# Binary-activation convolution: thresholds moved from VectorE to GpSimd, eviction order and a PSUM bank changed

## The chip, the cores and the metric

The kernel runs on one core of a Trainium2 chip. The metric is the device time of one execution in microseconds. The kernel before took 206.68 us, the median of 3 runs (206.48 to 207.05). Engines are called PE (TensorE), DVE (VectorE), ACT (ScalarE), POOL (GpSimd) and SP (the DMA issuer).

## The reference

`x` has the shape 32 x 56 x 56 x 32 (images, height, width, channels), fp32. Each channel of each image is normalised over its 56 x 56 positions. The 3x3x32x32 filter is replaced by a sum of five sign filters, whose weights `alpha` solve a 5x5 least-squares system. Three sign activations of the normalised input, with thresholds shifted by `v[n]`, are convolved with it, scaled by `beta[n]`, summed, and added to the input:

```python
mean, std = jnp.mean(W), jnp.sqrt(jnp.var(W))
B = jnp.sign(W[None] - mean + us[:, None, None, None, None] * std)      # 5 sign filters
alpha = jnp.linalg.solve(Bf.T @ Bf, Bf.T @ wf)
W_eff = jnp.einsum('m,mhwio->hwio', alpha, B)
for n in range(3):
    An = jnp.sign(jnp.clip(X + v[n], 0.0, 1.0) - 0.5)                   # X: x normalised per image and channel
    out = out + beta[n] * (conv(An) + sum(alpha) * bias[n])
return x + out
```

The sign of `clip(X + v, 0, 1) - 0.5` is the sign of `x` minus a threshold per image and channel. So the kernel never writes the normalised input; it needs a mean, a deviation and three thresholds for every image and channel.

## The kernel before

The 32 images are 16 pairs. A pair is loaded with its 112 rows (2 images x 56) on the partitions and transposed on PE, so that four columns x 32 channels lie on the partitions. Each pair has two halves of blocks, 8 and 6; a half fills two PSUM banks of `x_ps`, `y_ps` or `conv_ps[f]` with 448 or 336 columns each.

For a pair, in this order:
- PE transposes x (`bring_in`, L685), ACT copies it to `x_ch` (`copy_in`, L343).
- DVE takes statistics per lane (L555, L562) and spreads them (L565). PE gathers them over the four lanes of a channel with one matmul (`gather_lanes`, L693), DVE aggregates the result to moments (L573), ACT takes the root (L353), DVE makes the reciprocal and three thresholds (L577 to L591).
- ACT takes the signs for activations 1, 2, 0 (L348), each in two instructions, one per image.
- DVE weighs the signs of activations 1 and 2 with high parts of the ratios of beta (L599, L601), adds them (L605), and adds the signs of activation 0 (L612). POOL weighs them with low parts (L306, L310), and DVE adds these (L617).
- SP copies the sums by DMA to `s_odd`, shifted over the partitions. PE convolves them (`convolve`, L723, L726, L731).
- ACT evicts with a scale (`scale_out`, L361), PE transposes back (`bring_out`, L743), DVE adds x and a constant (L546), SP stores.

Every engine runs a list written out by hand, `step(p)` for p from -2 to 15; in one step pair p is finished, pair p+1 begins its convolution, pair p+2 is summed, pair p+3 gets its thresholds and first signs, and pair p+4 is brought in. Engines meet by semaphores only. The order on PE is convolve(p, 1), bring_out(p, 0), bring_in(p+4, 0), gather_lanes(p+3), convolve(p+1, 0), bring_out(p, 1), bring_in(p+4, 1). On ACT it is signs 2 of p+2, scale_out(p, 1), signs 0 of p+2, root of p+3, both copies of p+4, signs 1 of p+3, scale_out(p+1, 0).

Ahead of the steps stand the filter's own work (mean, signs, Gram matrix, elimination, `filter_parts` at L501) and the order of the activations by the size of beta on POOL (`order_beta`, L249; `split_ratios`, L277). The parameters beta, v and bias come by three DMAs that broadcast them to 128 partitions. `filter_parts` weighs the five sign filters one after another (L506 to L516).

The gathered statistics `stat_ps` lie in columns 464 to 487 of the first bank of `x_ps`.

Of the kernel before, what the change touches and what calls it, by code (L numbers as in the profile page):

```python
# [36 lines left out]
def preact_conv_kernel(nc, x, w, beta, v, bias, out):  # L37
    ctx = ExitStack()
    with ctx:
# [28 lines left out]
        twice_dev = sb("twice_dev", [128, 2])  # L68
# [8 lines left out]
        eps_col = sb("eps_col", [128, 1])  # L77
        params = sb("params", [128, 3, N_ACT])
# [21 lines left out]
        size = sb("size", [128, 3])  # L100
        w_eff = sb("w_eff", [128, TAPS, 2, C])
# [22 lines left out]
        root_ready = sem("root_ready")  # L124
        thr_ready = sem("thr_ready")
# [19 lines left out]
        bias_loaded = sem("bias_loaded")  # L145
# [86 lines left out]
        def _(pool):  # L232
# [16 lines left out]
            def order_beta():  # L249

                pool.wait_ge(params_loaded, 32)
# [66 lines left out]
            weigh_low(0)  # L318
            pool.wait_ge(lo_weighed, 2)
# [5 lines left out]
            for q in range(1, PAIRS):  # L325
                weigh_low(q)

        @block.scalar
        def _(act):
            load_filter(act, 1)  # L330
            act.dma_start(params[:, 1, :], v.partition_broadcast(128)).then_inc(params_loaded, 16)
            act.dma_start(params[:, 0, :], beta.partition_broadcast(128)).then_inc(params_loaded, 16)
            act.dma_start(params[:, 2, :], bias.partition_broadcast(128)).then_inc(bias_loaded, 16)
# [30 lines left out]
            def begin_signs(q):  # L364
                act.wait_ge(thr_ready, 3 * (q + 1))
# [9 lines left out]
            def step(p):  # L375
# [4 lines left out]
                if real(p + 2):  # L380
                    sign(p + 2, 0)
                if real(p + 3):
                    take_root(p + 3)
                if real(p + LEAD):
                    copy_in(p + LEAD, 0)
                    copy_in(p + LEAD, 1)
                if real(p + 3):
                    begin_signs(p + 3)
                if p == -1:
                    act.wait_ge(y_scale_ready, 1)  # L390
                if real(p + 1):
                    scale_out(p + 1, 0)

# [10 lines left out]
            copy_in(1, 0)  # L404
            copy_in(1, 1)
            begin_signs(0)
# [4 lines left out]
        def _(dve):  # L411
# [89 lines left out]
            def filter_parts():  # L501
                neg_w = w_eff[:].rearrange("p a o c -> p (a o c)")
                fl = [filt[:, :, :, :, m].rearrange("p a o c -> p (a o c)") for m in range(M_FIL)]
# [5 lines left out]
                mark(nc.vector.reciprocal(size[:, 1:2], size[:, 0:1]))  # L509
# [12 lines left out]
                dve.wait_ge(bias_loaded, 16)  # L522
                dve.wait_ge(params_loaded, 32)
# [51 lines left out]
            def invert_root(q):  # L575
                dve.wait_ge(root_ready, q + 1)
                return mark(nc.vector.reciprocal(inv_root[:], root[:]))  # L577

            def divide_variance(q, n):
                dve.wait_ge(moments_ready, 2 * (q + 1))  # L580
                settle(n)
                return mark(stt(twice_dev[:], moments[q % 2][:, :, 1], GN_EPS, inv_root[:], ALU.add, ALU.mult))  # L582

            def add_root(n):
                settle(n)
                return mark(tt(twice_dev[:], twice_dev[:], root[:], ALU.add))

            def make_thresholds(q, n):
                settle(n)
                for m in range(N_ACT):  # L590
                    stt(neg_thr[q % 2][:, m, :], twice_dev[:], order[:, 1, m:m + 1], moments[q % 2][:, :, 0],  # L591
                        ALU.mult, ALU.subtract).then_inc(thr_ready, 1)

            def thresholds(q):
                make_thresholds(q, add_root(divide_variance(q, invert_root(q))))
# [23 lines left out]
            def step(p):  # L619
# [10 lines left out]
                if real(r):  # L630
                    make_thresholds(r, add_root(divide_variance(r, invert_root(r))))
# [14 lines left out]
            filter_bias()  # L646
            lane_moments(0, 0)
# [4 lines left out]
            dve.wait_ge(divisor_ready, 1)  # L652
            nc.vector.reciprocal(tmp[:, 5, 2:3], tmp[:, 5, 1:2]).then_inc(inverse_ready, 1)
            dve.wait_ge(order_ready, 3)
            thresholds(0)
# [158 lines left out]
```

## Time and profile before

| | |
|---|---|
| median of the runs | 206.68 us |
| profiled execution | 206.35 us, span 204.6 us |
| PE busy | 167.0 us, 82% |
| DVE busy | 171.6 us, 84% |
| ACT busy | 139.9 us, 68% |
| POOL busy | 62.7 us, 31% |
| chain that ended last | PE 49%, ACT 19%, DVE 16%, issue 7%, DMA 6% |

The span is the time from the first to the last instruction of the profiled execution; the execution's own time is longer by 1.75 us. Busy shares are averages over a start of some 45 us, a middle in which all engines repeat a period, and a tail of some 40 us. The chain that ended last is followed back from the last instruction, at each step to what released it.

### The profile page before, as it was taken

The page shows a single profiled execution, that of the slowest core. Times are in us where ns is not written, and L with a number is a line of the kernel's source. Part 1 is how long each engine was busy: PE and PEld are TensorE (multiplying, and loading weights), DVE is VectorE, ACT ScalarE, POOL GpSimd, SP SyncE. Part 2 cuts the span into 40 slices and gives each one's busy share as a digit, 9 for nine tenths or more (in the row PEclk, how much of TensorE's full clock was granted, in tenths as well). Part 3 has the DMA queues.
Part 4 walks back from the last instruction along what each step waited for, and adds up shares of the span by engine and source line. Part 5 has one row for each costly group of instructions (what it writes and reads, how often), then busy time and mean ns, then how long its engine had stood idle before and what let it go on. Part 6 is the DMA issues. An engine that isn't in the chain of part 4 may idle for free.

```text
span 204.6 us, 4766 instructions
## 1 busy us (share of the span) xinstructions
PE 167.0 (82%) x1800; PEld 128.9 (63%) x1800; DVE 171.6 (84%) x422; ACT 139.9 (68%) x183; POOL 62.7 (31%) x76
## 2 busy tenths in 40 slices
PE   1596166489898989898989898989899999789871
PEld 0484065266767676767676767777777776658560
DVE  5449999998999999999999999999999999875241
ACT  2626557287888878787878787878787878673110
POOL 6174243543333333232323232414141414240000
PEclk9999999999999999999999999999999999999998
DMA  4799333061688979797889787978797464657625
GB/s 113 228 268 272 94 81 85 0 163 51 193 233 240 265 215 262 212 256 221 239 240 262 216 254 226 255 224 253 227 251 229 131 187 137 181 149 211 194 67 157
DMA packets 21030, 39.61 MB, mean 194 GB/s; under 512 B 9744, under 2 KB 9744, under 8 KB 21008
## 3 DMA queue, kind: packets, MB, share of 16 engines
q1 hardware_dynamic: 20272, 39.27, 67.9%
q8 instruction: 14, 0.23, 0.5%
q10 hardware_dynamic: 736, 0.04, 0.2%
q14 instruction: 8, 0.07, 0.1%
HBM read 13.15 MB, written 12.85 MB: 127 GB/s over the span
## 4 chain that ended last, share of the span: by engine, by line
PE 49%; ACT 19%; DVE 16%; issue 7%; DMA 6%; SPq 2%; ACTq 0%; DVEq 0%
PE conv_ps L723 24%; PE y_ps L743 13%; ACT signs L348 13%; PE x_ps L685 9%; ACT y_ch L361 6%; DMA x_nat<-in_x 4%; DMA s_odd<-s_even 3%; DVE raw_stats L555 2%; DVE y_nat L546 2%; DVE twice_dev L582 1%; DVE s_even L612 1%; DVE s_even L617 1%; PE x_ps L693 1%; DVE neg_thr L591 1%; PE conv_ps L782 1%
## 5 line engine op out<-in xcount | busy, mean ns | idle before, releaser
L723 PE MATMUL conv_ps<-s_even,w_mm 128*64 128x448 f16 (+1 forms) x576 | 102.9, 332 | 3.0 <-DVE w_mm L518 1.6
L726 PE MATMUL conv_ps<-s_odd,w_mm 128*64 128x448 f16 (+2 forms) x576 | 102.9, 320 | 0.0
L348 ACT ACTIVATE signs<-x_ch,neg_thr 128x784 f16<-128x784 f32 x96 | 85.0, 940 | 2.2 <-DVE neg_thr L591 2.2
L723 PEld LDWEIGHTS conv_ps<-s_even,w_mm 128*64 128x64 f16 x576 | 60.5, 110 | 30.4 <-issue 5.0
L726 PEld LDWEIGHTS conv_ps<-s_odd,w_mm 128*64 128x64 f16 x576 | 60.6, 110 | 0.0
L546 DVE SCALAR_TENSOR_TENSOR y_nat<-y_ps,y_const,x_nat 112x1024 f32<-112x1024 f32 (+1 forms) x32 | 36.6, 1145 | 10.2 <-PE y_ps L743 10.2
L306 POOL TENSOR_SCALAR lo_part<-signs,ratio_lo 128x1568 f16<-128x1568 f16 x16 | 25.5, 1595 | 62.3 <-ACT signs L348 62.2
L685 PE MATMUL x_ps<-ident,x_nat 112*128 112x112 f32 x224 | 31.8, 290 | 13.4 <-ACT x_ch L343 10.1
L743 PE MATMUL y_ps<-ident,y_ch 128*112 128x128 f32 x224 | 31.2, 279 | 11.3 <-ACT y_ch L361 9.9
L310 POOL TENSOR_SCALAR lo_part<-signs,ratio_lo 128x1568 f16<-128x1568 f16 x16 | 26.6, 1664 | 44.9 <-DVE half_hi L605 44.9
L343 ACT ACTIVATE x_ch<-x_ps 128x896 f32<-128x896 f32 (+1 forms) x32 | 26.1, 815 | 19.5 <-PE x_ps L685 19.5
L361 ACT ACTIVATE y_ch<-conv_ps,y_scale 128x896 f32<-128x896 f32 (+1 forms) x32 | 28.9, 904 | 11.3 <-PE conv_ps L726 6.2
L685 PEld LDWEIGHTS x_ps<-ident,x_nat 112*128 112x128 f32 x224 | 27.1, 159 | 14.4 <-issue 12.1
L743 PEld LDWEIGHTS y_ps<-ident,y_ch 128*112 128x112 f32 x224 | 23.4, 133 | 20.0 <-ACT y_ch L361 12.6
L555 DVE BATCH_NORM_STATS2 raw_stats<-x_ch 128x6 f32<-128x448 f32 (+1 forms) x64 | 31.6, 553 | 4.0 <-ACT x_ch L343 4.0
L731 PE MATMUL conv_ps<-s_odd,w_edge 128*64 128x112 f16 x144 | 22.5, 214 | 0.0
L612 DVE TENSOR_TENSOR s_even<-half_hi,signs 128x1568 f16<-128x1568 f16 x16 | 19.6, 1226 | 0.0
L353 ACT ACTIVATE root<-moments,eps_col 128x2 f32<-128x2 f32 x16 | 4.7, 296 | 20.2 <-DVE moments L573 20.2
L605 DVE TENSOR_TENSOR half_hi<-hi_part 128x1568 f16<-128x1568 f16 x16 | 15.6, 976 | 0.6
L731 PEld LDWEIGHTS conv_ps<-s_odd,w_edge 128*64 128x64 f16 x144 | 15.6, 108 | 0.0
L617 DVE TENSOR_TENSOR s_even<-lo_part 128x1568 f16<-128x1568 f16 x16 | 15.5, 969 | 0.0
L601 DVE TENSOR_SCALAR hi_part<-signs,ratio_hi 128x1568 f16<-128x1568 f16 x16 | 10.0, 628 | 6.0 <-ACT signs L348 6.0
(106 smaller groups left out, 92.5 us busy)
## 6 DMA issues: line engine op xcount, KB each, us to landing
x_nat<-in_x SPq DMA_DIRECT2D x16, 448.0 KB, 5.1
out<-y_nat SPq DMA_DIRECT2D x16, 448.0 KB, 3.8
s_odd<-s_even SPq DMA_DIRECT2D x32, 203.0 KB, 2.8
s_odd<-s_even SPq DMA_DIRECT2D x32, 188.5 KB, 3.0
x_nat<-in_x SPq DMA_DIRECT2D x16, 336.0 KB, 4.7
out<-y_nat SPq DMA_DIRECT2D x16, 322.0 KB, 2.6
s_odd<-s_even SPq DMA_DIRECT2D x32, 14.5 KB, 2.7
x_nat<-in_x SPq DMA_DIRECT2D x16, 14.0 KB, 5.3
```

The source lines that it names most:

```text
L306: ts(lo_part[0][:], signs[q % 2][:, 1].rearrange("p i a h -> p (i a h)"), ratio_lo[:, 0:1], 1.0, ALU.mult, ALU.mult).then_inc(lo_weighed, 1)
L310: ts(lo_part[1][:], signs[q % 2][:, 2].rearrange("p i a h -> p (i a h)"), ratio_lo[:, 1:2], 1.0, ALU.mult, ALU.mult).then_inc(lo_weighed, 1)
L343: act.activation(to.rearrange("p (b n) -> p b n", b=2), x_ps[:, :, 0:n], ACT.Copy).then_inc(x_copied, 1)
L348: act.activation(signs[q % 2][:, n, :, a, :], x_ch[q % CH_SLOTS][:, :, a, :], ACT.Sign, bias=neg_thr[q % 2][:, n, a:a + 1]).then_inc(signe ...
L361: act.activation(y_ch[f][:].rearrange("p (b n) -> p b n", b=2), conv_ps[f][:, :, 0:n], ACT.Copy, scale=y_scale[:]).then_inc(y_scaled, 1)
L546: stt(y_nat[b][:, at:at + 2 * n].rearrange("p (b n) -> p b n", b=2), y_ps[0:ROWS, :, 0:n], y_const[0:ROWS, :], x_nat[p % X_SLOTS][:, C + a ...
L555: mark(nc.vector.bn_stats(raw_stats[q % 2][:, a, f, :], x_ch[q % CH_SLOTS][:, i.start:i.stop, a, :]))
L685: last = nc.tensor.transpose(x_ps[:, j // PER_BANK[f], at:at + ROWS], x_nat[s][:, 128 * i:128 * (i + 1)], ident[0:ROWS, 0:ROWS])
L723: last = nc.tensor.matmul(low[:, 0:n * ROWS], wt, s_even[b][:, part, r0:r0 + 2 * n, t:t + H], start=first, stop=end)
L726: last = nc.tensor.matmul(high[:, 0:m * ROWS], wt, s_odd[b][:, part, r0:r0 + 2 * m, t:t + H], start=first, stop=end and not at_edge)
L731: last = nc.tensor.matmul(high[:, m * ROWS:n * ROWS], we, s_odd[b][:, part, r0 + 2 * m:r0 + 2 * n, t:t + H], start=False, stop=end)
L743: last = nc.tensor.transpose(y_ps[0:ROWS, j // PER_BANK[f], at:at + 128], y_ch[f][:, j * ROWS:(j + 1) * ROWS], ident[:])
```

## The change

- Thresholds: VectorE keeps the reciprocal (`invert_root`); the variance product, the addition of the root, and the three thresholds are five linked GpSimd operations (`thresholds`). On POOL they follow the second low-part product of the pair before. ACT waits for one count of `thr_ready` in place of three.
- ACT's order: the first copy of p+4 ahead of the root; scale_out(p+1, 0) ahead of the second copy and of signs 1. In step -1, signs 1 of pair 2 stand ahead of scale_out(0, 0).
- `stat_ps` lies in the first bank of `conv_ps[1]`. So `gather_lanes(q)` waits until scale_out(q-3, 1) is done, and `convolve(p, 1)` until the moments of pair p+2 are taken.
- Parameters: three loads of one row, spread by a PE matmul with ones, copied by DVE. On POOL the order of beta stands behind the clearing of the filter's corners.
- `filter_parts`: one product over all five filters and one reduction.
- Startup order: the divisor's reciprocal behind two eliminations, the gathering of pair 0 ahead of the transposes of pair 1, signs 1 of pair 0 ahead of the second copy of pair 1.

```diff
-        stat_ps = x_ps[:, 0, 464:464 + 6 * G]
+        stat_ps = conv_ps[1][:, 0, 464:464 + 6 * G]
+        params_ps = conv_ps[1][:, 0, 0:3 * N_ACT]
...
-                pool.wait_ge(params_loaded, 32)
+                pool.wait_ge(params_ready, 1)
...
+            def thresholds(q):
+                mom = moments[q % 2]
+                pool.wait_ge(moments_ready, 2 * (q + 1))
+                link(ts(twice_dev[:, 0, :], mom[:, :, 1], GN_EPS, 1.0, ALU.add, ALU.mult))
+                pool.wait_ge(inv_ready, q + 1)
+                link(tt(twice_dev[:, 1, :], twice_dev[:, 0, :], inv_root[:], ALU.mult))
+                link(tt(twice_dev[:, 2, :], twice_dev[:, 1, :], root[:], ALU.add))
+                link(tt(scaled_dev[:], twice_dev[:, 2:3, :].broadcast_to([128, N_ACT, 2]),
+                        order[:, 1, :].unsqueeze(2).broadcast_to([128, N_ACT, 2]), ALU.mult))
+                tt(neg_thr[q % 2][:], scaled_dev[:], mom[:, :, 0].unsqueeze(1).broadcast_to([128, N_ACT, 2]),
+                   ALU.subtract).then_inc(thr_ready, 1)
...
-            weigh_low(0)
-            pool.wait_ge(lo_weighed, 2)
+            order_beta()
+            thresholds(0)
+            split_ratios()
+            pool.wait_ge(ratios_ready, 3)
+            pool.wait_ge(thr_ready, 1)
+            weigh_low_first(0)
+            weigh_low_second(0)
+            thresholds(1)
+            pool.wait_ge(thr_ready, 2)
             pool.wait_ge(w_ready, 3)
...
             for q in range(1, PAIRS):
-                weigh_low(q)
+                weigh_low_first(q)
+                weigh_low_second(q)
+                if real(q + 1):
+                    thresholds(q + 1)
...
+                if real(p + LEAD):
+                    copy_in(p + LEAD, 0)
                 if real(p + 3):
                     take_root(p + 3)
-                if real(p + LEAD):
-                    copy_in(p + LEAD, 0)
-                    copy_in(p + LEAD, 1)
-                if real(p + 3):
-                    begin_signs(p + 3)
                 if p == -1:
+                    begin_signs(2)
                     act.wait_ge(y_scale_ready, 1)
                 if real(p + 1):
                     scale_out(p + 1, 0)
+                if real(p + LEAD):
+                    copy_in(p + LEAD, 1)
+                if real(p + 3) and p != -1:
+                    begin_signs(p + 3)
...
-                link(ts(neg_w, fl[0], neg_alpha[:, 0:1], None, ALU.mult))
+                link(tt(w_parts[:], fl, neg_alpha.unsqueeze(1).broadcast_to([128, TAPS * 2 * C, M_FIL]), ALU.mult))
                 mark(nc.vector.reduce_sum(size[:, 0:1], w_stat[:, 6:11], axis=AX.X))
-                link(stt(neg_w, fl[1], neg_alpha[:, 1:2], neg_w, ALU.mult, ALU.add))
+                link(nc.vector.reduce_sum(neg_w, w_parts[:], axis=AX.X))
...
-                    make_thresholds(r, add_root(divide_variance(r, invert_root(r))))
+                    invert_root(r)
...
                 pe.wait_ge(lanes_ready, q + 1)
                 if q:
                     pe.wait_ge(moments_ready, 2 * q)
+                if real(q - 3):
+                    pe.wait_ge(y_scaled, 2 * (q - 3) + 2)
...
+                if f == 1:
+                    pe.wait_ge(moments_ready, 2 * min(p + 3, PAIRS))
...
+            pe.wait_ge(params_loaded, 48)
+            nc.tensor.matmul(params_ps, ones[0:1, :], params_row[:].rearrange("p i n -> p (i n)"),
+                             start=True, stop=True).then_inc(params_spread, 1)
...
-            bring_in(1, 0)
             gather_lanes(0)
...
+            bring_in(1, 0)
             bring_in(1, 1)
```

## Rows read from the trace of the kernel before

**Rows 1.** The chain of waits over one period: start us, us, what.

```profile
104.28 1.78 ACT signs L348 x2
106.05 0.91 ACT y_ch L361
...
107.00 1.09 PE y_ps L743 x8
...
112.58 0.80 PE y_ps L743 x6
...
114.61 1.78 ACT signs L348 x2
```

**Rows 2.** The windows, one row per stretch: busy us of each engine, granted clock, DMA.

```profile
104.28:114.62 10.34, 9.71 (x115) 7.44 (x111) 9.74 (x23) 8.47 (x13) 3.14 (x2) 1.00 0.85 247
```

**Rows 3.** The timeline of ACT in that period: start us, us, engine, line, operation.

```profile
106.84 1.78 ACT L348 ACTIVATE signs<-x_ch,neg_thr 128x784 f16<-128x784 f32 x2
108.52 0.81 ACT L361 ACTIVATE y_ch<-conv_ps,y_scale 128x672 f32<-128x672 f32 x1
...
113.99 0.73 ACT L343 ACTIVATE x_ch<-x_ps 128x672 f32<-128x672 f32 x1 [1.16 <-PE x_ps L685]
```

**Rows 4.** The timeline of PE and its weight loads around the gathering matmul L693.

```profile
21.77 0.62 PE L693 MATMUL x_ps<-spread_stats,same_ch 128*128 128x24 f32 x2 [1.63 <-DVE spread_stats L565]
...
108.60 0.30 PEld L693 LDWEIGHTS x_ps<-spread_stats,same_ch 128*128 128x128 f32 x2
108.94 0.11 PEld L723 LDWEIGHTS conv_ps<-s_even,w_mm 128*64 128x64 f16 x1
```

**Rows 5.** The timeline of POOL and DVE late in that period.

```profile
110.47 1.57 POOL L310 TENSOR_SCALAR lo_part<-signs,ratio_lo 128x1568 f16<-128x1568 f16 x1 [2.75 <-DVE half_hi L605]
...
111.61 1.25 DVE L612 TENSOR_TENSOR s_even<-half_hi,signs 128x1568 f16<-128x1568 f16 x1
112.78 0.15 DVE L577 RECIPROCAL inv_root<-root 128x2 f32<-128x2 f32 x1
...
113.84 1.01 DVE L546 SCALAR_TENSOR_TENSOR y_nat<-y_ps,y_const,x_nat 112x768 f32<-112x768 f32 x1
```

**Rows 6.** The timeline of POOL in the start.

```profile
9.17 0.19 POOL L252 COPY tmp<-params 128x3 f32<-128x3 f32 x1 [5.13 <-DMA params<-in_L_conv_beta]
...
14.35 0.23 POOL L278 TENSOR_SCALAR tmp<-order 128x1 f32<-128x1 f32 x1
...
16.66 0.49 POOL L315 MEMSET filt<- 32x480 f32 x1
...
26.04 2.30 POOL L310 TENSOR_SCALAR lo_part<-signs,ratio_lo 128x1568 f16<-128x1568 f16 x1 [4.35 <-DVE half_hi L605]
```

**Rows 7.** The timeline of DVE in the start.

```profile
20.54 1.18 DVE L565 TENSOR_TENSOR spread_stats<-own_group,lane_stats 128x24 f32<-128x24 f32 x1
...
24.89 0.97 DVE L605 TENSOR_TENSOR half_hi<-hi_part 128x1568 f16<-128x1568 f16 x1
...
27.09 1.26 DVE L582 SCALAR_TENSOR_TENSOR twice_dev<-moments,inv_root 128x2 f32<-128x2 f32 x1
...
28.98 0.97 DVE L617 TENSOR_TENSOR s_even<-lo_part 128x1568 f16<-128x1568 f16 x1
...
30.44 0.55 DVE L508 SCALAR_TENSOR_TENSOR w_eff<-filt,neg_row,w_eff 128x192 f32<-128x192 f32 x1
...
33.05 0.32 DVE L518 TENSOR_SCALAR w_mm<-w_eff,size 128x192 f16<-128x192 f32 x1
...
38.04 0.98 DVE L605 TENSOR_TENSOR half_hi<-hi_part 128x1568 f16<-128x1568 f16 x1
```

**Rows 8.** The timeline of ACT in the start.

```profile
8.26 1.01 ACT L373 ACTIVATE filt<-w_raw,w_bias 128x192 f32<-128x192 f32 x2
...
52.59 1.78 ACT L348 ACTIVATE signs<-x_ch,neg_thr 128x784 f16<-128x784 f32 x2
```

**Rows 9.** The chain of waits in the tail.

```profile
181.71 0.35 PE conv_ps L723
```

More of the change, by code:

```diff
@@ L67, in preact_conv_kernel @@
         inv_root = sb("inv_root", [128, 2])
-        twice_dev = sb("twice_dev", [128, 2])
+        twice_dev = sb("twice_dev", [128, 3, 2])
+        scaled_dev = sb("scaled_dev", [128, N_ACT, 2])
         neg_thr = [sb(f"neg_thr{i}", [128, N_ACT, 2]) for i in range(2)]
@@ L77, in preact_conv_kernel @@
         eps_col = sb("eps_col", [128, 1])
+        params_row = sb("params_row", [1, 3, N_ACT])
         params = sb("params", [128, 3, N_ACT])
@@ L100, in preact_conv_kernel @@
         size = sb("size", [128, 3])
+        w_parts = sb("w_parts", [128, TAPS * 2 * C, M_FIL])
         w_eff = sb("w_eff", [128, TAPS, 2, C])
@@ L124, in preact_conv_kernel @@
         root_ready = sem("root_ready")
+        inv_ready = sem("inv_ready")
         thr_ready = sem("thr_ready")
@@ L144, in preact_conv_kernel @@
         params_loaded = sem("params_loaded")
-        bias_loaded = sem("bias_loaded")
+        params_spread = sem("params_spread")
+        params_ready = sem("params_ready")
         w_loaded = sem("w_loaded")
@@ L330, in _ @@
             load_filter(act, 1)
-            act.dma_start(params[:, 1, :], v.partition_broadcast(128)).then_inc(params_loaded, 16)
-            act.dma_start(params[:, 0, :], beta.partition_broadcast(128)).then_inc(params_loaded, 16)
-            act.dma_start(params[:, 2, :], bias.partition_broadcast(128)).then_inc(bias_loaded, 16)
+            for i, t in enumerate((beta, v, bias)):
+                act.dma_start(params_row[:, i, :], t.unsqueeze(0)).then_inc(params_loaded, 16)
             def copy_in(q, f):
@@ L364, in begin_signs @@
             def begin_signs(q):
-                act.wait_ge(thr_ready, 3 * (q + 1))
+                act.wait_ge(thr_ready, q + 1)
                 if real(q - 2):
@@ L404, in _ @@
             copy_in(1, 0)
+            begin_signs(0)
             copy_in(1, 1)
-            begin_signs(0)
             for p in range(-2, PAIRS):
@@ L502, in filter_parts @@
                 neg_w = w_eff[:].rearrange("p a o c -> p (a o c)")
-                fl = [filt[:, :, :, :, m].rearrange("p a o c -> p (a o c)") for m in range(M_FIL)]
+                fl = filt[:].rearrange("p a o c m -> p (a o c) m")[:, :, 0:M_FIL]
                 dve.wait_ge(corners_zero, 2)
                 mark(stt(w_stat[:, 6:11], neg_alpha, -1.0, neg_alpha, ALU.mult, ALU.max))
-                link(ts(neg_w, fl[0], neg_alpha[:, 0:1], None, ALU.mult))
+                link(tt(w_parts[:], fl, neg_alpha.unsqueeze(1).broadcast_to([128, TAPS * 2 * C, M_FIL]), ALU.mult))
                 mark(nc.vector.reduce_sum(size[:, 0:1], w_stat[:, 6:11], axis=AX.X))
-                link(stt(neg_w, fl[1], neg_alpha[:, 1:2], neg_w, ALU.mult, ALU.add))
-                mark(nc.vector.reciprocal(size[:, 1:2], size[:, 0:1]))
+                link(nc.vector.reduce_sum(neg_w, w_parts[:], axis=AX.X))
+                link(nc.vector.reciprocal(size[:, 1:2], size[:, 0:1]))
+                link(ts(size[:, 2:3], size[:, 1:2], -W_SCALE, None, ALU.mult))
                 dve.wait_ge(order_ready, 3)
@@ L576, in invert_root @@
                 dve.wait_ge(root_ready, q + 1)
[L577 to L595, printed above, removed]
+                if q:
+                    dve.wait_ge(thr_ready, q)
+                nc.vector.reciprocal(inv_root[:], root[:]).then_inc(inv_ready, 1)
             def weigh_high(q):
@@ L646, in _ @@
             filter_bias()
+            dve.wait_ge(params_spread, 1)
+            nc.vector.tensor_copy(params[:].rearrange("p i n -> p (i n)"), params_ps).then_inc(params_ready, 1)
             lane_moments(0, 0)
@@ L651, in _ @@
             pair_moments(0)
[L652 to L655, printed above, removed]
+            invert_root(0)
             dve.wait_ge(gram_summed, 1)
@@ L659, in _ @@
             eliminate(1)
+            dve.wait_ge(divisor_ready, 1)
+            nc.vector.reciprocal(tmp[:, 5, 2:3], tmp[:, 5, 1:2]).then_inc(inverse_ready, 1)
             lane_moments(1, 0)
```

12 lines of the change are left out of this document (2 added, 10 removed).

## The prediction

> **What bounds the kernel now.** I read the windows first, then the chain of waits over one period, then the timeline of each engine there, then start and tail. From 52 to 166 us the kernel repeats every 10.34 us, with one row like that of [rows 2] for each of eleven periods: PE busy 9.71, DVE 9.74, ACT 8.47, POOL 3.14, granted clock 1.00. No engine is full, so a loop of waits sets the period. [rows 1] shows it. Write S1, S2, S0 for the signs of activations 1, 2 and 0, O0 and O1 for the evictions of the two conv halves (L361), C0 and C1 for the copies of transposed x (L343), B0, B1, I0, I1 for the transposes out and in, G for the gathering matmul (L693). The loop is S1, O0, B0, I0, G, first conv half, B1, I1, C1, and S1 of the next pair 10.33 later. PE stands still in it once, ahead of B0, while it waits for O0, which stands behind S1 on ACT.
>
> DVE is nearly as full, and the thresholds lie on it: from the reciprocal at 112.78 to the addition at 113.84 [rows 5].
>
> **Part 1, the loop.** O0 goes ahead of C1 and S1. The conv half that it reads ends near 112.58 and C1 began at 113.99 [rows 1, 3], so O0 (0.91) fits in ACT's idle time there and costs nothing; were C1 ready at once, it would cost 0.91. PE's wait ahead of B0 goes. What is late next? G now writes the bank that O1 reads, and waits for O1 of pair p (y_scaled 2(q-3)+2), with the whole first conv half of pair p+1 queued behind it on PE; on ACT, O1 stands behind S1 and S2. The new loop is S1, S2, O1, G, conv half, B1, I1, C1, S1:
> - S1 and S2: 1.68 each (106.84 to 108.52 is S2) [rows 3]: 3.36
> - O1: 0.81 [rows 3]; release of PE 0.04 (O0 ended at 106.96, B0 began at 107.00 [rows 1])
> - G from its weight load to the conv's first load: 108.94 - 108.60 = 0.34 [rows 4]
> - from there to the next S1: 114.61 - 108.94 = 5.67 [rows 1, 4]
>
> Sum 10.22, against 10.34: only 0.12 less. The wait moves from B0 to G and does not go; PE would allow about 9.7 and DVE about 9.1. What the trace does not show is a G in the steady part that begins from a stop, and its path to the next conv load. Below I take 0.24 (its two loads lie 0.30, and the next may run ahead by a part); above 0.62, the whole of the one G that did begin from a stop [rows 4], in the slow start. I take 0.34, the row in place; with both ends the period is 10.12 to 10.50.
>
> The second conv half also waits for the moments of pair p+3: these come after A0 (the first addition), near 6.5 after S1, and that half starts at 9.6. Free.
>
> **Part 2, thresholds on POOL.** DVE loses five small operations, some 0.8 us of its period, and has nothing to do with it: A1 then waits for B1, which ended at 113.38, 9.10 after S1 [rows 1]; less 0.12 that is 8.98, where it started at 9.56. POOL gets five linked operations. Its small ones in [rows 6] are 0.19 to 0.3 each; 9.17 to 14.35 holds 18 of them, mean 0.29. I take 1.4 for five. In a steady period POOL's second product starts near S1 + 5.3, lasts 1.57, and DVE's L612 waits for it: 111.61 plus 1.25 ends 0.82 after POOL's 112.04 [rows 5]. The reciprocal then comes near 7.7, the thresholds at 9.3, S1 is due at 10.2. Covered by 0.9; without that cover each period pays the excess.
>
> In the two ramp steps there is no such cover. POOL must first do L310, and DVE's L617 wakes at the same moment. The trace shows the two engines excluding each other: L565, 24 elements, took 1.18 at 20.54, and L582, two elements, took 1.26 and ended at 28.35, where L310 (26.04 + 2.30) ends [rows 6, 7].
>
> The Trainium skill (SBUF — State Buffer, section "Who interferes with whom") says that a DVE instruction with two SBUF inputs and a GpSimd instruction that reads SBUF exclude each other, and the later one waits for the whole of the other. The two rows above agree. By that rule each new POOL operation can hold up L617, and be held up by it; without it S1 of pair 2 would come 0.9 sooner, and the total would be 205.7.
>
> **Part 3, startup.** The order chain on POOL no longer waits for the broadcast parameters (9.17), but for the last filter sign (8.26 + 1.01 = 9.27 [rows 8]) and two memsets of 0.5 [rows 6]: it starts at 10.4, lasts 5.2, thresholds 1.4, so S1 of pair 0 starts at 17.0. The parameters now are three one-row loads, a matmul and a copy, wanted by POOL at 10.4. The broadcasts were there at 9.17 [rows 6]; even rows as late as that cost POOL nothing, and PE's first transposes, queued behind them, perhaps 1. DVE waits for the divisor to 17.5, the ratios come at 19.1, POOL's first product then ends at 20.8, and L565 is free of it there instead of at 21.7 [rows 7]. So the first L605 is 0.8 earlier, at 24.1 for 24.89. L310 behind it ends 3.45 later (24.89 to 28.34 [rows 6, 7]); one POOL operation of 0.25 may go ahead of L617, which starts at 27.8. Before, L582 and the thresholds held it to 28.98 [rows 7]: 1.2 earlier.
>
> filter_parts: five linked combinations of 192 elements, from L617's end (28.98 + 0.9) to 33.05 [rows 7] 3.2 us, become one product and one reduction of 960 elements each. Bounds of such a pass: 0.55 for 192 elements in L508 is 2.1 ns each beside a fixed 0.15, so 2.2 us; L605's 0.97 for 1568 halves is 0.6 ns each, so 0.75. I take 1.5 for the product and 1.2 for the reduction with its one input, between the ends, and 0.7 for the small steps now in series: 3.4, 0.2 longer (0.5 shorter to 0.9 longer, if one of the two is off). The second L605 starts at 38.04 - 1.2 + 0.2 = 37.0 [rows 7].
>
> From it: L310 ends 3.45 later (40.5); one threshold operation 0.25, L617 0.9, the other four 1.1 and a release 0.1: S1 of pair 2 at 42.8. Behind it in the new order come O0 (0.91) and C1 (0.62) ahead of S2 (the special case p == -1), then 3.36 of signs, 0.81, 0.04, 0.34, 5.67: S1 of pair 3 at 54.5, where it was at 52.59 [rows 8]. **Start: +1.9**, between +0.5 (thresholds unhindered, short product) and +2.6.
>
> **Part 4, steady.** Eleven periods to S1 of pair 14: 11 x -0.12 = **-1.3** (bounds -2.4 and +1.8).
>
> **Part 5, tail.** The last low parts reach PE by DMA: PE was released at 181.71 [rows 9], by L617 behind A1. A1 comes 9.56 - 8.98 = **0.6 earlier** relative to its S1; the rest of the chain (second shift, evictions, stores) is as before.
>
> **Sum.** +1.9 - 1.3 - 0.6 = 0.0 on the profiled execution (span 204.6, time 206.35); the median of the runs shown is 206.68. I forecast 206.6 us. The least difference that a measurement of this kernel can tell is about 0.3%, 0.6 us.
>
> **Rivals.**
> - The ramp is cheaper or the loop shorter: the threshold operations slip in behind L617 without its 0.9, or G costs 0.24. The first alone gives +1.0 - 1.3 - 0.6, the second +1.9 - 2.4 - 0.6: -1.0 either way, 205.6 us; both, 204.6. For it: POOL's operations are linked and leave gaps. Against: the two lockouts of [rows 7].
> - The gate on O1 takes all that the eviction gained. The decisive place is G: it can no longer load its weights under I0's matmuls. From 0.46 (load and matmul in series) the period is 10.34, the steady part gives nothing, and start and tail remain: 206.6 + 1.3 = 207.9 us; at 0.5 it is 208.3, at 0.62 209.7. For it: the 0.62 of [rows 4]. Against: B0 began from a stop with no visible loss [rows 1]. This one is slower.
> - Thresholds become the loop: if the five operations take over 2.3 in place of 1.4, or L612 takes the port later, S1 waits every period. At 0.3 too late each, 11 x 0.3 = 3.3: 210 us. Little speaks for it at 0.2 to 0.3 an operation.
> - PE wins its whole idle time: G finds O1 done, and the period is 9.7: 11 x -0.6 and the start, 200 us. That needs O1 ahead of the signs, which the order does not have.
> - Slower ramp of another kind (late parameter rows ahead of PE's first transposes, or the first conv half at half rate because PE now stands idle longer after its warming matmuls): +1, 207.6 us.
>
> **How the numbers follow.** Forecast (205.9 to 207.3 by itself) 0.42; cheaper ramp or loop 0.25; gate 0.15; slower ramp 0.10; thresholds 0.05; PE-bound 0.03. Faster by over 0.3% is under 206.06: the second and last, and 0.07 of the forecast's low end: 0.35. Slower, over 207.30: gate, ramp, thresholds and 0.01 of the forecast: 0.31. Between: 0.34. The range 204.8 to 208.6 leaves out PE-bound, late thresholds and the ends of the others.
>
> **What would show it.** Right: the period is near 10.2; PE's idle time stands ahead of G and is put down to ACT's L361, none ahead of B0; ACT's S1 follows C1 at once; DVE waits for B1 before A1; S1 of pair 3 near 54.5. Wrong: a period under 10.0 (the gate isn't the loop), L348 waiting for POOL in steady periods, S1 of pair 2 before 42, or a first conv half with matmuls of more than 0.2 spacing.

## The result, and the profile after

The changed kernel took 219.5 us, the median of 4 runs (218.23 to 221.02), against 206.58 for the kernel before on the same chip: a ratio of 1.064, 95% interval 1.055 to 1.072. The profiled execution took 219.92 us, its span is 218.1, 13.5 more than before.

Line numbers are those of the kernel whose trace is shown, so they shift by a few between runs. In the changed kernel L321 and L327 are POOL's two low-part products (L306 and L310 before), L308 to L314 its five threshold operations, L588 DVE's spread of the statistics (L565), L606 and L608 its two weighings (L599, L601), L619 and L624 its sums (L612, L617), and L569 the additions to the output (L546; A0 and A1 for the two halves).

The windows of the changed kernel, one steady period, then from signs 1 of pair 1 to those of pair 2, from there to those of pair 3, and the slow part of that (columns as in [rows 2]):

```profile
102.84:113.92 11.08, 9.85 (x117) 7.47 (x114) 10.10 (x18) 8.69 (x12) 6.38 (x7) 1.00 0.79 223
32.26:43.85 11.59, 8.90 (x89) 6.05 (x89) 9.77 (x28) 6.25 (x8) 6.57 (x9) 0.85 0.16 40
43.85:57.67 13.82, 11.00 (x76) 7.54 (x78) 7.28 (x15) 10.10 (x14) 4.72 (x7) 0.75 0.33 93
48.00:54.00 6.00, 5.91 (x33) 3.58 (x33) 5.26 (x12) 4.31 (x6) 2.75 (x4) 0.51 0.22 64
```

The period is 11.08 where [rows 2] has 10.34. POOL's busy time doubled, 3.14 to 6.38, and five operations of 0.2 cannot do that. The first group of the page that is new shows where: one 128x6 subtraction, 16 times.

```profile
L314 POOL TENSOR_TENSOR neg_thr<-scaled_dev,moments 128x6 f32<-128x6 f32 x16 | 23.1, 1447 | 1.3
L374 ACT ACTIVATE signs<-x_ch,neg_thr 128x784 f16<-128x784 f32 x96 | 83.9, 937 | 19.5 <-POOL neg_thr L314 19.5
```

ACT stood still 19.5 us in all, waiting for it: 0.68 in each steady period, and 10.3 before 60 us in the start. The chain of waits over one period answers to [rows 1]; POOL, which was not in it, is now on it:

```profile
117.24 1.69 ACT signs L374 x2
...
120.03 1.17 DVE s_even L619
...
121.42 0.20 POOL twice_dev L310
...
122.25 1.88 POOL neg_thr L314
```

The chain follows semaphores, so it says only that L314 was long. Why shows in DVE's timeline of the same stretch, against POOL's (columns as in [rows 5]), with ACT's row for signs 1 and 2 of this period behind them:

```profile
115.21 1.34 DVE L588 TENSOR_TENSOR spread_stats<-own_group,lane_stats 128x24 f32<-128x24 f32 x1
...
117.01 0.62 DVE L608 TENSOR_SCALAR hi_part<-signs,ratio_hi 128x1568 f16<-128x1568 f16 x1
...
119.95 1.25 DVE L619 TENSOR_TENSOR s_even<-half_hi,signs 128x1568 f16<-128x1568 f16 x1
121.12 0.15 DVE L602 RECIPROCAL inv_root<-root 128x2 f32<-128x2 f32 x1
122.17 1.02 DVE L569 SCALAR_TENSOR_TENSOR y_nat<-y_ps,y_const,x_nat 112x768 f32<-112x768 f32 x1 [0.89 <-PE y_ps L755]
123.10 0.97 DVE L624 TENSOR_TENSOR s_even<-lo_part 128x1568 f16<-128x1568 f16 x1
```

```profile
114.95 1.57 POOL L321 TENSOR_SCALAR lo_part<-signs,ratio_lo 128x1568 f16<-128x1568 f16 x1 [1.92 <-ACT signs L374]
...
118.81 1.57 POOL L327 TENSOR_SCALAR lo_part<-signs,ratio_lo 128x1568 f16<-128x1568 f16 x1 [2.28 <-DVE half_hi L612]
120.47 0.79 POOL L308 TENSOR_SCALAR twice_dev<-moments 128x2 f32<-128x2 f32 x1
121.42 0.20 POOL L310 TENSOR_TENSOR twice_dev<-twice_dev,inv_root 128x2 f32<-128x2 f32 x1 [0.17 <-DVE inv_root L602]
121.70 0.19 POOL L311 TENSOR_TENSOR twice_dev<-twice_dev,root 128x2 f32<-128x2 f32 x1
121.97 0.20 POOL L312 TENSOR_TENSOR scaled_dev<-twice_dev,order 128x6 f32<-128x6 f32 x1
122.25 1.87 POOL L314 TENSOR_TENSOR neg_thr<-scaled_dev,moments 128x6 f32<-128x6 f32 x1
```

```profile
113.07 3.47 ACT L374 ACTIVATE signs<-x_ch,neg_thr 128x784 f16<-128x784 f32 x4 [0.68 <-POOL neg_thr L314]
```

Of POOL's five linked operations three took 0.2. The first, L308, took 0.79: it ended at 121.26, just behind L619 (121.20), which had been running since before it. That cost nothing, because the reciprocal that the second operation waits for was there only at 121.27. The last began 0.08 after DVE's second addition (L569, called A1 in the prediction) and ended at 124.12, just after the sum behind A1 (L624, the old L617) ended at 124.07. So the real loop is S1 at 113.07, 9.10 to A1's start, 0.93 to L624's start, 0.97 of L624, 0.08 to S1 of the next pair: 11.08.

The account of the 13.5 us, from the starts of signs 1:

| | before | after | difference |
|---|---|---|---|
| S1 of pair 3 | 52.59 [rows 8] | 57.67 | +5.1 |
| eleven periods | 113.71 | 121.90 | +8.2 |
| S1 of pair 14 to the end | 38.30 | 38.53 | +0.2 |

```profile
43.85 1.79 ACT L374 ACTIVATE signs<-x_ch,neg_thr 128x784 f16<-128x784 f32 x2 [4.06 <-POOL neg_thr L314]
...
57.67 3.46 ACT L374 ACTIVATE signs<-x_ch,neg_thr 128x784 f16<-128x784 f32 x4
...
179.57 3.47 ACT L374 ACTIVATE signs<-x_ch,neg_thr 128x784 f16<-128x784 f32 x4 [0.68 <-POOL neg_thr L314]
```

### The profile page after: what moved, and what is told of

Its sections match the earlier page's. It is cut to its first block, busy times and chain, and to the rows that moved or that the text cites. A ratio compares the mean times of both kernels' runs of the same rounds, so it can differ in the third digit from the quotient of the medians.

```text
span 218.1 us, 4801 instructions
## 1 busy us (share of the span) xinstructions
PE 174.7 (80%) x1802; PEld 132.2 (61%) x1802; DVE 169.9 (78%) x340; ACT 142.8 (65%) x183; POOL 109.5 (50%) x156
## 4 chain that ended last, share of the span: by engine, by line
ACT 32%; DVE 19%; POOL 19%; issue 15%; PE 9%; DMA 3%; ACTq 1%; SPq 1%; DVEq 0%; POOLq 0%
ACT signs L374 26%; POOL neg_thr L314 10%; DVE s_even L619 7%; ACT y_ch L387 5%; PE conv_ps L735 4%; DVE y_nat L569 2%; PE y_ps L755 2%; PE x_ps L693 2%; DMA params_row<-in_L_conv_bias 2%; POOL lo_part L327 2%; DVE moments L596 2%; POOL scaled_dev L312 1%; POOL twice_dev L310 1%; POOL twice_dev L311 1%; DVE raw_stats L578 1%
## 5 line engine op out<-in xcount | busy, mean ns | idle before, releaser
L735 PE MATMUL conv_ps<-s_even,w_mm 128*64 128x448 f16 (+1 forms) x576 | 106.3, 339 | 5.1 <-DVE w_mm L543 3.2
L738 PE MATMUL conv_ps<-s_odd,w_mm 128*64 128x448 f16 (+2 forms) x576 | 106.2, 327 | 0.0
L374 ACT ACTIVATE signs<-x_ch,neg_thr 128x784 f16<-128x784 f32 x96 | 83.9, 937 | 19.5 <-POOL neg_thr L314 19.5
L735 PEld LDWEIGHTS conv_ps<-s_even,w_mm 128*64 128x64 f16 x576 | 61.7, 112 | 34.6 <-issue 10.2
L738 PEld LDWEIGHTS conv_ps<-s_odd,w_mm 128*64 128x64 f16 x576 | 61.8, 112 | 0.0
L569 DVE SCALAR_TENSOR_TENSOR y_nat<-y_ps,y_const,x_nat 112x1024 f32<-112x1024 f32 (+1 forms) x32 | 36.7, 1148 | 23.6 <-PE y_ps L755 23.6
L327 POOL TENSOR_SCALAR lo_part<-signs,ratio_lo 128x1568 f16<-128x1568 f16 x16 | 26.7, 1669 | 39.5 <-DVE half_hi L612 39.5
L321 POOL TENSOR_SCALAR lo_part<-signs,ratio_lo 128x1568 f16<-128x1568 f16 x16 | 25.6, 1599 | 30.2 <-ACT signs L374 30.0
L693 PE MATMUL x_ps<-ident,x_nat 112*128 112x112 f32 x224 | 32.4, 293 | 6.3 <-ACT x_ch L369 6.3
L693 PEld LDWEIGHTS x_ps<-ident,x_nat 112*128 112x128 f32 x224 | 28.0, 163 | 7.3 <-issue 7.3
L314 POOL TENSOR_TENSOR neg_thr<-scaled_dev,moments 128x6 f32<-128x6 f32 x16 | 23.1, 1447 | 1.3
L619 DVE TENSOR_TENSOR s_even<-half_hi,signs 128x1568 f16<-128x1568 f16 x16 | 19.6, 1226 | 0.0
L703 PE MATMUL conv_ps<-spread_stats,same_ch 128*128 128x24 f32 x32 | 6.7, 289 | 15.3 <-ACT y_ch L387 14.7
L624 DVE TENSOR_TENSOR s_even<-lo_part 128x1568 f16<-128x1568 f16 x16 | 15.5, 970 | 2.7 <-POOL lo_part L327 2.7
L703 PEld LDWEIGHTS conv_ps<-spread_stats,same_ch 128*128 128x128 f32 x32 | 5.4, 211 | 18.5 <-DVE spread_stats L588 16.5
L588 DVE TENSOR_TENSOR spread_stats<-own_group,lane_stats 128x24 f32<-128x24 f32 x16 | 16.2, 1011 | 0.6
```

Source lines behind the costliest of these rows:

```text
L314: tt(neg_thr[q % 2][:], scaled_dev[:], mom[:, :, 0].unsqueeze(1).broadcast_to([128, N_ACT, 2]), ALU.subtract).then_inc(thr_ready, 1)
L327: ts(lo_part[1][:], signs[q % 2][:, 2].rearrange("p i a h -> p (i a h)"), ratio_lo[:, 1:2], 1.0, ALU.mult, ALU.mult).then_inc(lo_weighed, 1)
L374: act.activation(signs[q % 2][:, n, :, a, :], x_ch[q % CH_SLOTS][:, :, a, :], ACT.Sign, bias=neg_thr[q % 2][:, n, a:a + 1]).then_inc(signe ...
L569: stt(y_nat[b][:, at:at + 2 * n].rearrange("p (b n) -> p b n", b=2), y_ps[0:ROWS, :, 0:n], y_const[0:ROWS, :], x_nat[p % X_SLOTS][:, C + a ...
L619: tt(inner(q, 0), rows(half_hi), signs[q % 2][:, 0].rearrange("p i a h -> p (i a) h"), ALU.add)\
L693: last = nc.tensor.transpose(x_ps[:, j // PER_BANK[f], at:at + ROWS], x_nat[s][:, 128 * i:128 * (i + 1)], ident[0:ROWS, 0:ROWS])
```

## Experiments

Eleven kernels. "Ratio" is each one's time to that of the kernel before on the same chip, with its 95% interval. S1(k) is the start of signs 1 of pair k.

**1. Thresholds back on VectorE, all else of the change kept.**

```diff
@@ POOL
-            thresholds(0)
...
-            thresholds(1)
...
-                    thresholds(q + 1)
@@ DVE
-                    invert_root(r)
+                    make_thresholds(r, add_root(divide_variance(r, invert_root(r))))
```

> The changed kernel with the five threshold operations back on DVE as in the kernel before; the PSUM bank, the gate of the gathering matmul, ACT's order, parameters and filter product stay as changed. Port theory (the last POOL operation stands still until DVE's L569 and L624 are done, and ACT's signs wait for it): the period falls from 11.08 to 10.2 to 10.3, the loop of the prediction; 11 periods give 9, the start about 1.5: 208.5 to 209.5 us. Gate theory (waiting for the eviction ahead of the gathering matmul costs the 0.75 per period by itself): the period stays near 11.1, 218 us.

Measured 208.22 us, ratio 1.004 (1.000 to 1.008); period 10.285; S1(2) at 43.22, S1(3) at 55.02; S1(14) to the end 37.8. By the ratios the threshold move is 0.060 of the 0.064, some 12 of the 13 us. Not all of that is the period (11 x 0.80 = 8.8): S1(3) comes 2.65 earlier, of which 2.0 lie in a stretch where TensorE had a higher clock in this run than in the changed kernel (see part 3 below). The rest of the prediction's loop stood: in its weight loads G's conv half begins 0.33 after G.

```profile
110.72 0.30 PEld L701 LDWEIGHTS conv_ps<-spread_stats,same_ch 128*128 128x128 f32 x2 [0.61 <-issue]
111.05 0.11 PEld L733 LDWEIGHTS conv_ps<-s_even,w_mm 128*64 128x64 f16 x1
```

**2. One of POOL's five operations left out** (the addition of the root, so its thresholds lack that term).

```diff
-                link(tt(twice_dev[:, 2, :], twice_dev[:, 1, :], root[:], ALU.add))
-                link(tt(scaled_dev[:], twice_dev[:, 2:3, :].broadcast_to([128, N_ACT, 2]),
+                link(tt(scaled_dev[:], twice_dev[:, 1:2, :].broadcast_to([128, N_ACT, 2]),
```

> The changed kernel with one of the five POOL operations left out, the addition of the root (0.27 us with its link); the thresholds are then another number, all else is as changed. Port theory: the last operation (now 0.27 earlier) is through before DVE's L569 starts 0.08 ahead of it at present, takes 0.20 in place of 1.87, and the period falls by 0.7 to 0.8, far more than what was left out: 210 to 211.5 us. Length theory (five linked operations are simply long): 0.27 per period, 11 x 0.27 = 3, 216.5 us. Gate theory: no change, 219.

Measured 208.49, ratio 1.006 (1.001 to 1.010), period 10.285. An operation of 0.27 with its gap gave back 0.80 per period, and the ratio fell from 1.064 to 1.006, by more than 10 us in all. No sum of durations does this; a threshold in time does. POOL's timeline, and DVE's: the last operation now begins 0.19 ahead of A1.

```profile
115.25 0.20 POOL L313 TENSOR_TENSOR neg_thr<-scaled_dev,moments 128x6 f32<-128x6 f32 x1
```

```profile
115.44 1.02 DVE L568 SCALAR_TENSOR_TENSOR y_nat<-y_ps,y_const,x_nat 112x768 f32<-112x768 f32 x1 [0.88 <-PE y_ps L754]
```

**3. Eighteen matmuls that nothing waits for, on PE ahead of the first transposes out**, against its slow clock in the start.

```diff
+                    if p == 0:
+                        for _ in range(18):
+                            nc.tensor.matmul(y_ps[:, 1, 0:128], ones[:], ones[:], start=True, stop=True)
```

> The changed kernel with 18 matmuls of ones (128x128, fp32, into a part of y_ps that is overwritten later) on PE between the second conv half of pair 0 and its transposes out, where PE stands idle for 4.3 us and then runs at half rate for 4 us. Clock theory: the granted clock of 43.85 to 57.67 rises from 0.75 to near 1, the first signs of pair 3 come 2.5 to 3 us earlier, total 216.5 to 217. If the half rate has another cause: 219.5 or somewhat more. Steady period unchanged at 11.08 by both.

Measured 218.82, ratio 1.053 (1.045 to 1.062). S1(3) at 55.74, 1.9 earlier, from S1(2) at 43.94; the period stayed 11.08. The gain in the start is less than the 2.5 to 3 us expected. In that stretch the clock was at the higher level throughout, where the changed kernel has 0.75:

```profile
43.50:55.70 12.20, 11.32 (x110) 9.23 (x110) 7.82 (x17) 10.05 (x13) 5.05 (x9) 1.00 0.45 124
```

This shows what the higher clock is worth there, 11.80 from S1(2) to S1(3) in place of 13.82. It doesn't show that the eighteen matmuls brought the clock back: experiments 2 and 6 have 1.00 and 11.8 in the same stretch without them.

**4. Experiment 1 with O1 ahead of signs 2.**

```diff
-                if real(p + 2):
-                    sign(p + 2, 2)
...
                     scale_out(p, 1)
+                if real(p + 2):
+                    sign(p + 2, 2)
```

> As the first kernel (thresholds on DVE), and on ACT the second-half eviction goes ahead of the second signs, so the gathering matmul no longer waits for two signs. Port theory with the loop of the prediction: the gate leaves the loop, PE alone would allow 9.7, DVE with its thresholds 9.95: period 9.9 to 10.1, total 204.5 to 206.5, 3 us under the first. Gate theory: the period falls from 11.1 to 9.9, 12 us under the first.

Measured 208.28, ratio 1.003 (0.999 to 1.008): a miss. Its periods alternate between 9.95 and up to 10.76, mean 10.15, and G then waits for DVE's spread of the statistics in eight of ten. The profiled execution took 210.96, well above its median, so I take no more from it than that the wait moved to DVE.

**5. The kernel before with only O0 moved ahead of C1 and signs 1**: statistics still in `x_ps`, thresholds on VectorE.

```diff
-                    copy_in(p + LEAD, 1)
-                if real(p + 3):
-                    begin_signs(p + 3)
...
                     scale_out(p + 1, 0)
+                if real(p + LEAD):
+                    copy_in(p + LEAD, 1)
+                if real(p + 3):
+                    begin_signs(p + 3)
```

> The kernel before with one thing of the change alone: on ACT the first-half eviction of pair p+1 goes ahead of the second copy of p+4 and of the first signs of p+3. The statistics stay in the bank of x_ps, so no gate on the gathering matmul; thresholds stay on DVE. If the gate had taken what the eviction gains (the loop reading): PE's wait ahead of the transposes out goes, DVE with 9.95 of work becomes the bound, period 10.0 in place of 10.34; 11 periods give 3.7, the ramp about 1 more: 202 to 203.5 us. If the eviction order is worth nothing: 206 to 207.

Measured 202.39, ratio 0.976 (0.970 to 0.982): faster than both. Periods 9.97 on average (51.90 to 161.57 over eleven), the chain 68% PE. So this order on ACT gains 0.37 a period. Experiment 1, with the same place of O0, has 10.285. In the steady period it differs from this kernel by the bank of the statistics with its gates and by the place of the root behind C0, and the gate is where its PE stands (the loop of part 1); no run has the bank change alone.

**6. The changed kernel with the sum L624 ahead of A1.**

```diff
-                if real(p):
-                    add_x(p, 1)
                 if real(q):
                     sum_low(q)
+                if real(p):
+                    add_x(p, 1)
```

> The changed kernel with DVE's L624 (two SBUF inputs) ahead of the second L569 (one PSUM and one SBUF input, and a scalar column in SBUF). Three or four of POOL's threshold operations then lie beside L569 alone. If L569 blocks a POOL TENSOR_TENSOR by itself: one of them takes about 1.0 and the period is 10.7, total 215. If only L624 blocks: L310 waits for L624 (0.8), the others take 0.20 each beside L569, period 10.3, total 211.

Measured 208.26, ratio 1.005 (1.000 to 1.011), period 10.285. POOL's timeline, then DVE's:

```profile
115.19 0.78 POOL L310 TENSOR_TENSOR twice_dev<-twice_dev,inv_root 128x2 f32<-128x2 f32 x1 [0.17 <-DVE inv_root L602]
116.04 0.19 POOL L311 TENSOR_TENSOR twice_dev<-twice_dev,root 128x2 f32<-128x2 f32 x1
116.31 0.20 POOL L312 TENSOR_TENSOR scaled_dev<-twice_dev,order 128x6 f32<-128x6 f32 x1
116.59 0.20 POOL L314 TENSOR_TENSOR neg_thr<-scaled_dev,moments 128x6 f32<-128x6 f32 x1
```

```profile
114.96 0.95 DVE L624 TENSOR_TENSOR s_even<-lo_part 128x1568 f16<-128x1568 f16 x1
115.92 1.02 DVE L569 SCALAR_TENSOR_TENSOR y_nat<-y_ps,y_const,x_nat 112x768 f32<-112x768 f32 x1
```

L310 ends when L624 ends (115.97 and 115.91). The three behind it run beside A1 at 0.19 to 0.20: A1, whose one tensor in SBUF is `x_nat`, holds nobody off. So what held L314 in the changed kernel was L624, while it was still queued behind A1.

**7. The changed kernel with O1 ahead of signs 2** (the edit of experiment 4).

> The changed kernel, thresholds on POOL, with the second-half eviction ahead of the second signs on ACT: the gathering matmul no longer waits for two signs. Port theory: POOL's last operation still falls on L569 and L624, signs still wait for it; the period stays at 10.8 to 11.3, total 217 to 221. Gate theory: the gate was the cost, period 10.0 and under, total 207.

Two runs, 220.59 and 225.01 us, too few for a ratio; the profile is that of the first, and its period is 11.19. The idea that the gate on O1 makes the 11.08 falls with it: with O1 early the period does not get shorter. POOL's and DVE's timelines:

```profile
109.91 1.70 POOL L310 TENSOR_TENSOR twice_dev<-twice_dev,inv_root 128x2 f32<-128x2 f32 x1 [0.17 <-DVE inv_root L602]
```

```profile
109.69 0.99 DVE L569 SCALAR_TENSOR_TENSOR y_nat<-y_ps,y_const,x_nat 112x768 f32<-112x768 f32 x1
110.60 0.96 DVE L624 TENSOR_TENSOR s_even<-lo_part 128x1568 f16<-128x1568 f16 x1
```

Now it is L310 that begins behind A1's start, 0.22 behind, and it is held to 111.61, the end of L624 at 111.56.

**8. The changed kernel with one wait more: DVE does not issue L624 before A1 is finished.**

```diff
                 dve.wait_ge(lo_weighed, 2 * (q + 1))
+                if real(q - 2):
+                    dve.wait_ge(y_added, 2 * (q - 2) + 2)
```

> The changed kernel with one wait more on DVE: L624 isn't started before the L569 ahead of it has finished (by its own semaphore). Nothing is taken away. Queue theory: DVE's L624, handed over behind the running L569, holds the shared port from then on, so POOL's last threshold operation (issued 0.08 after L569 starts) waits for both; with the wait the port is free during L569, that operation takes 0.2 in place of 1.87, the period falls to 10.3: 208 to 210 us. If L569 itself holds the port, or the wait merely delays DVE: the operation takes 1.0 or more, the period is 11.1 or longer, 219.5 to 221.

Measured 210.65, ratio 1.013 (1.008 to 1.019), period 10.29. POOL's timeline, then DVE's:

```profile
116.57 0.20 POOL L314 TENSOR_TENSOR neg_thr<-scaled_dev,moments 128x6 f32<-128x6 f32 x1
```

```profile
116.48 1.02 DVE L569 SCALAR_TENSOR_TENSOR y_nat<-y_ps,y_const,x_nat 112x768 f32<-112x768 f32 x1 [0.88 <-PE y_ps L757]
...
117.60 0.98 DVE L626 TENSOR_TENSOR s_even<-lo_part 128x1568 f16<-128x1568 f16 x1
```

The last operation begins 0.09 behind A1's start, as in the changed kernel, and takes 0.20 where it took 1.87. The added wait costs DVE 0.2 (the two ran into each other by 0.09 before, and stand 0.10 apart now) and takes 0.79 off the period. The ratio goes from 1.064 to 1.013, some 10 us. This is the decisive run: same operations, same order, only the time at which L624 is issued.

**9. Experiment 5 with the thresholds of pairs 3 and up on POOL, no added wait.**

```diff
+                if q >= 2 and real(q + 1):
+                    thresholds(q + 1)
...
+                    if r < 3:
+                        make_thresholds(r, add_root(divide_variance(r, invert_root(r))))
+                    else:
...
+                        nc.vector.reciprocal(inv_root[:], root[:]).then_inc(inv_ready, 1)
```

> The kernel before with the first-half eviction ahead (as e5_before_o0) and the thresholds of pairs 3 and up on POOL, statistics in x_ps, no gate. DVE has 9.1 of work, PE 9.7. Queue theory: POOL's last operations fall beside L624's predecessor and are held through L624 in every period, signs wait, period 10.3 to 10.8: 205 to 210 us. If they slip in ahead of it: 9.75, 200 us.

Measured 210.98, ratio 1.015 (1.009 to 1.021); the period is 10.67 where experiment 5 has 9.97. In another kernel, with another order on ACT, the same thing shows: below, L310 begins 0.22 behind A1's start (61.88) and ends with the sum queued behind A1 (63.75). In nine of eleven periods one operation is held so. In the other two the last operation begins ahead of A1, as in experiment 2, and the four behind the reciprocal take 0.20. POOL's timeline:

```profile
62.10 1.70 POOL L310 TENSOR_TENSOR pool_dev<-pool_dev,inv_root 128x2 f32<-128x2 f32 x1 [0.17 <-DVE inv_root L654]
```

**10. Experiment 9 with the wait of experiment 8.**

> As e9_pool_late with DVE's wait between the second output addition and the low sum. Queue theory: the threshold operations pass beside the addition, period 9.7 to 9.8, PE the bound: 199 to 200.5 us, under e5_before_o0. If the wait doesn't free the port: as e9_pool_late, and 0.1 per period more.

Measured 200.59 (200.29 to 202.78), ratio 0.969 (0.962 to 0.976): the fastest kernel here: 6.9 us below the kernel before on the same chip (207.52), 10.4 below experiment 9. All POOL operations behind the reciprocal take 0.20, and PE is full; the windows, then POOL's timeline:

```profile
110.00:120.00 10.00, 10.00 (x118) 7.68 (x115) 9.56 (x19) 8.72 (x13) 5.06 (x8) 1.00 0.92 267
```

```profile
112.27 0.20 POOL L314 TENSOR_TENSOR neg_thr<-scaled_dev,moments 128x6 f32<-128x6 f32 x1
```

The period is 9.70 (64.13 to 161.14 over ten), which the prediction gave as PE's limit.

**11. Experiment 1 without the special order of ACT in step -1.**

```diff
                 if p == -1:
-                    begin_signs(2)
...
-                if real(p + 3) and p != -1:
+                if real(p + 3):
```

> As e1_thr_dve (changed kernel, thresholds on DVE) with ACT's special order in step -1 taken back: eviction of pair 0 and second copy of pair 3 stand ahead of the first signs of pair 2, as in all other steps. If that order is part of the startup's loss: the first signs of pair 3 start 1.3 to 1.8 earlier (53.3 to 53.7 for 55.0), PE's idle stretch ahead of its first transposes out is shorter, total 206.5. If it isn't: 208.

Measured 208.34, ratio 1.003 (0.999 to 1.007), S1(3) at 55.67: a miss. The windows show the granted clock at 0.86 in the stretch that was at 1.00 in experiment 1, so the run does not say what the order by itself is worth.

```profile
44.00:56.00 12.00, 9.99 (x88) 6.65 (x85) 10.15 (x23) 8.62 (x12) 3.15 (x2) 0.86 0.50 139
```

## Why the prediction was wrong

The forecast was 206.6 with 204.8 to 208.6; 219.5 is outside. The step that failed is the one in part 2 that ends "Covered by 0.9". Measured less forecast on the profiled execution, the 13.5 us are 8.8 from the held thresholds, 0.7 from the loop (10.285 for 10.22), 3.2 from the start and 0.8 from the tail.

**Part 2, thresholds: wrong, 9 of the 13 us.** The operations behind the reciprocal were sized well: unheld they are 0.2 each, 0.27 with the gap. From L310's start to L314's start, 0.83 in the changed kernel, and 0.2 more, they would end at S1 + 9.38, where S1 is due at + 10.29. So the cover was there by durations, 0.9. What I did not do is apply to the steady period the exclusion that I had read in [rows 7] and used for the start. My own numbers had the clash: thresholds from 7.7 to 9.3, A1 at 8.98, and L617 right behind it. Had I asked whether a POOL operation meets L617 while that one runs, these numbers would have answered no, since L617 would have begun near 9.9. It need not run. It is enough that it is queued: experiment 6 frees A1 of blame, 7 moves the hold to another POOL operation, and 8 takes only the queueing away. The rival "Thresholds become the loop" had the right form and the right sign, with 0.3 per period where 0.80 was paid (11.08 less the 10.285 of experiments 1, 2, 6 and 8), and a chance of 0.05. The price of a late operation is no matter of how late it is: experiment 2 shows 0.27 us of work turning into 0.80 per period.

The reciprocal stood at S1 + 8.05 where I had 7.7, because POOL's second product began 5.74 behind S1, not 5.3 (118.81 in the rows above). With L314 only 0.08 on the wrong side of A1's start, 0.35 less would have put it ahead of A1, as in experiment 2. The 0.44 is the same exclusion the other way round. DVE's spread at 115.21, 1.34 long for 0.18 before, is held by POOL's first product until 116.52, and the weighings behind it come late: signs 2 were out at 116.54, but their weighing (L608) began at 117.01, where the kernel before began it 0.04 behind the signs (108.66 for 108.62). Without the hold it could have begun near 116.58, and the second product 0.43 earlier. This is an estimate from the rows; no run takes the hold away.

The Trainium skill (SBUF — State Buffer, section "Who interferes with whom") says, in its point on DVE's two-port modes, "Whoever issues first gets the shared pair for the whole instruction; the other **fully blocks**". I read that as who starts first. In the changed kernel L314's record starts 0.85 before L624's and still L314 is the one that waits, 1.87. For this pair of instructions the trace agrees with the sentence only if a DVE instruction counts as issued while it is queued behind a running one, which experiment 8 supports: 0.20 once it is held back by a semaphore.

**Part 1, the loop: right.** Predicted 10.22, measured 10.285 wherever POOL did not hold the signs (experiments 1, 2, 6 and 8). Its terms are 3.36, 0.80, 0.12 for PE's release where I had 0.04, 0.33 for G, 5.68 from there. That O0's new place is worth more where the statistics stay in `x_ps` is shown by experiment 5: 9.97.

**Part 3, the start: the terms were right in kind, their sizes were not, and one path was missed.** S1(0) came at 17.75 for 17.0, S1(2) at 43.85 for 42.8, S1(3) at 57.67 for 54.5. Of the first 1.1, then, 0.75 is there at S1(0). The traces show where it comes from. The parameters' matmul stands ahead of PE's first transposes, which began at 6.38 for 5.67 before; the prediction had that as "perhaps 1" for PE and nothing for POOL. But ACT copies the transposes before it makes the last filter signs, so these ended at 10.01 for 9.27, and POOL's order chain, which waits for them, began at 11.23 for the 10.4 worked out. Behind S1(0) the product took 1.89 where I had 1.5, the reduction 1.14 for 1.2, and the lockouts foreseen for this stretch came, one more than I had counted; DVE's timeline, then POOL's:

```profile
28.47 0.98 DVE L624 TENSOR_TENSOR s_even<-lo_part 128x1568 f16<-128x1568 f16 x1 [1.40 <-POOL lo_part L327]
...
29.44 1.89 DVE L534 TENSOR_TENSOR w_parts<-filt,neg_row 128x960 f32<-128x960 f32 x1
...
31.45 1.14 DVE L536 TENSOR_REDUCE w_eff<-w_parts 128x192 f32<-128x960 f32 x1
```

```profile
28.52 0.97 POOL L308 TENSOR_SCALAR twice_dev<-moments 128x2 f32<-128x2 f32 x1
29.58 1.82 POOL L310 TENSOR_TENSOR twice_dev<-twice_dev,inv_root 128x2 f32<-128x2 f32 x1
```

L308 ends with L624 (29.49 and 29.45), L310 with the product L534 (31.40 and 31.33). With the thresholds on DVE (experiment 1) S1(2) is 0.6 earlier.

The other 2.1 lie between S1(2) and S1(3): predicted 11.7, measured 13.8, but 11.80 in experiments 1 and 3, where the clock was at 1.00. So the working was right for a PE at the higher clock. In the changed kernel PE stood still from 42.50 to 46.59, waiting for O0, which in this step stands behind S1(2) on ACT, and then ran at half rate: granted clock 0.51 from 48 to 54 us, the lower of its levels (1.2 GHz, not 2.4). PE's timeline has the conv's matmuls 0.38 apart at first and 0.19 apart later:

```profile
42.29 0.21 PE L743 MATMUL conv_ps<-s_odd,w_edge 128*64 128x112 f16 x1
46.59 0.66 PE L755 MATMUL y_ps<-ident,y_ch 128*112 128x128 f32 x4 [4.08 <-ACT y_ch L387]
...
50.20 0.58 PE L735 MATMUL conv_ps<-s_even,w_mm 128*64 128x448 f16 x1
...
50.58 0.58 PE L735 MATMUL conv_ps<-s_even,w_mm 128*64 128x448 f16 x1
...
54.13 0.35 PE L735 MATMUL conv_ps<-s_even,w_mm 128*64 128x448 f16 x1
...
54.32 0.35 PE L735 MATMUL conv_ps<-s_even,w_mm 128*64 128x448 f16 x1
```

The rival "slower ramp" named this and gave it +1 and 0.10. Between kernels that differ little the clock from S1(2) to S1(3) was 0.75 (the changed one), 1.00 (experiments 1, 2, 3 and 6) and 0.86 (experiments 8 and 11). The length of PE's stop alone doesn't decide it: PE stood still 3.46 us ahead of B0 in experiment 2 and kept 1.00, and 2.55 us in experiment 8 and lost it for a while.

**Part 5, the tail.** Predicted -0.6. It is -0.5 in experiment 1 (37.8 for 38.3) and +0.2 in the changed kernel: the term was about right, and in the changed kernel it did not show, since the thresholds were held there too (S1 of the last pair comes 11.08 after that of pair 14, for 9.21 in experiment 1).

**Still open.** What decides in which kernel PE loses its clock; whether POOL's one-input products are held by a queued DVE instruction in the same way, which no run here isolates; and what the hold on DVE's spread costs, which is only estimated above.

## What to carry to other kernels

A small operation with two SBUF inputs, moved to POOL, can last as long as what DVE has in line. Look, at the time at which it will be issued, for a DVE instruction with two SBUF inputs, be it the running one or the one behind it, and count up to its end, not POOL's own 0.2. If one is in line, reorder DVE or let it wait before it issues that instruction (by a reordering 11.08 to 10.285, by a wait 11.08 to 10.29 and 10.67 to 9.70 us per period here). And when a cover comes out of durations alone, test it once more with every exclusion that the trace has shown elsewhere.

## What the runs showed of the hardware

A DVE instruction that has not begun already holds POOL off: L314 of the changed kernel waited through 0.85 us in which DVE ran only A1, beside which the same operation takes 0.20 when something else (experiment 6) or nothing (experiment 8) is queued. And a semaphore wait added to a busy engine took 0.79 us off each period in experiment 8 (ratio 1.013 for 1.064), and made the kernel of experiment 9 10.4 us faster in experiment 10, on the same chip.
